# A scan kernel on one core: at step 3 of each unit TensorE sums the last state of the unit before ahead of delta's products, and ScalarE copies y behind the decay of chunk 4

## The chip, the cores and the metric

One core of a Trainium2 chip runs the whole kernel. The metric is the device time of one execution in microseconds; 3 executions of the kernel before were timed.

## The reference, cut to what matters

A bidirectional state-space block over 4 sequences of 1024 tokens with 1024 inner channels and N = 16 states. For each direction (z is the projected input of the direction, B and C come from a small projection):

```
delta = softplus(Wdt @ dlt + bdt)
h[t]  = exp(delta * A_n) * h[t-1] + delta * B_n * z      (n = 0..15, scan over t)
y     = sum over n of (C_n * h) + Dp * z
out   = Wf @ (silu(mx) * (y1 + y2)) + bf + skip ; result = x + gate * out
```

## The kernel before, in words

A set-up part of about 260 us makes the normalised tokens, folded weights and projections. The rest is 64 **units**, k = 0..63: unit k is one tile of 128 channels of one direction of one sequence, with all 1024 tokens in the free dimension. Units come in groups of 8 (one sequence and direction). Each unit has 16 **steps**, c = 0..15, one for each state n; q = 16 k + c numbers them through and "chunk" c is the work of state c. Each engine has its own list, written out by hand in the loops `for k ... for c`, and works it strictly in order; the lists meet at semaphores.

The way a state's inflow (delta B z) is made depends on the letter of `KINDS = "EVEVAVAPAVAPAPAV"`: for E TensorE multiplies by a diagonal into `slot` (L900), for A ScalarE scales `dut` into `abuf` (L1123, `scale_half`) and TensorE transposes that into `slot` (L888, `turn_inflow`), for V and P GpSimd multiplies a loaded B by `du` into `bst` (L1222). For E and A the decay goes into the one buffer `dec`, for V and P into `slot`. In each step:

- ScalarE makes the decay exp(delta A_n) (L1184). For an E or A chunk it first waits until the scan of the E or A chunk before has read `dec`.
- VectorE scans (L1314); for V it also multiplies by C (L1319), for the others GpSimd does (L1227).
- TensorE sums: `sum_chunk(q - LAG)`, LAG = 4, adds the transposed product of four steps ago into the PSUM tile `y` (L877, 8 transposes of 128x128). A scan waits until the sum five chunks back has left its buffer in `hbuf` (HR = 5).

So the sums of chunks 12 to 15 of unit k-1 stand in steps 0 to 3 of unit k. Behind the last of them `copy_y(k-1)` on ScalarE moves `y` to `yrd` (L1114, waits for the semaphore `summed`), and only then `skip_terms(k)` on TensorE (L870, step 4, waits for `y_read`) may start the next `y`, in front of the sum of chunk 0. The next unit's delta is prepared meanwhile: `delta_product(k+1)` in step 3 (L837, four products of 512 columns into the PSUM tile `mb`, each half waiting for the last user of its half of `mb`), on ScalarE `softplus_start` in step 4 (L1079 and L1081) and `softplus_end` in step 5 (L1085), on VectorE `finish_delta` in step 5 (L1248).

What else lies in the first steps depends on the unit. Units 2-9, 18-25, 34-41 and 50-57 follow one in which the gate branch was made (`has_mx`, L858, sigmoid on ScalarE L1098 to L1106, silu L1268). Units 26-33, 42-49 and 58-63, and unit 17, follow one whose output projection spans the border: 32 products of 128 columns in step 15 and 32 in step 0 (L958, L963), read by L1284. Units 10-15 have 8 products of 512 columns of a small projection in the same places (L951, L1154). The first unit of a group (8, 16, 24, ...) makes a new diagonal on ScalarE (L1139). In unit 63 there is no delta to prepare, and further projections stand in steps 1 to 4.

ScalarE's list around the change, for one step c:

```python
nc.scalar.activation(decays, delta[:, k % 2, :], ACT.Exp, ...)      # decay of chunk c
if c in SCALE_STEPS: scale_half(...)
...
if c == LAG - 1 and k > 0: copy_y(k - 1)                            # step 3
if k + 1 < NU:
    if c == 4: softplus_start(k + 1)
    if c == 5: softplus_end(k + 1)
```

Of the kernel before, what the change touches and what calls it, by code (L numbers as in the profile page):

```python
# [24 lines left out]
NU = 2 * B * ET  # L25
# [456 lines left out]
LAG = 4  # L482
# [5 lines left out]
def kind(q):  # L488

    return KINDS[q % N]
# [20 lines left out]
def ssm_kernel(nc, t, scratch):  # L513

    with ExitStack() as ctx:
# [67 lines left out]
        def gates(k):  # L583

            return k > 0 and backward(k - 1)

        def has_mx(k):
            return not gates(k) and k % (2 * ET) != 0

        def mx_index(k):  # L590

            return k // (2 * ET) * ET + (ET - 1 if backward(k) else k % ET - 1)
# [8 lines left out]
        def dbc_job(k):  # L601

            return k - ET - 1 if ET < k < ET + 1 + NC - 2 else None
# [220 lines left out]
        def _(pe):  # L824
            def delta_product(k):
                pe.wait_ge(wdt_in[k % 2], 16 * (k // 2 + 1))
                pe.wait_ge(dl_in, 48 * (k // ET + 1))
                for h in range(2):
                    if k >= 2 and has_mx(k - 2):
                        pe.wait_ge(silu_ready, 2 * mx_index(k - 2) + h + 1)  # L830
                    elif k >= 2 and dbc_job(k - 2) is not None:
                        pe.wait_ge(dbc_ready, 2 * dbc_job(k - 2) + h + 1)
                    elif k >= 2 and h == 0 and projection_of(k - 2) is not None:
                        pe.wait_ge(proj_read, projection_of(k - 2) + 1)
                    elif k >= 1:
                        pe.wait_ge(dut_ready, 2 * k - 1 + h)
                    nc.tensor.matmul(mb[h], wdt[:, k % 2, :], dl[:, half(h)], start=True, stop=True).then_inc(dps_mm, 1)  # L837
# [36 lines left out]
            def sum_chunk(q):  # L874
                wait_product(pe, q)
                for j in range(ET):
                    last = nc.tensor.matmul(y[:, j * P:(j + 1) * P], hbuf[:, q % HR, j * P:(j + 1) * P], ident[:],  # L877
                                            start=False, stop=(q % N == N - 1), is_transpose=True,
                                            skip_group_check=True)
                last.then_inc(summed, 1)  # L880
# [127 lines left out]
            for k in range(NU):  # L1008
                e, zs = k % ET, z_step(k)
                new_b = (k + 1) % ET == 0  # L1010
                for c in range(N):
                    q = N * k + c
                    if kind(q) == "A":
                        turn_inflow(q)
                    elif kind(q) == "E":
                        spread_inflow(q)
                    if c == 3 and k + 1 < NU:
                        delta_product(k + 1)
                    if c == LAG:
                        skip_terms(k)  # L1020
                    if q >= LAG:
                        sum_chunk(q - LAG)
                    if c == 0 and k > 0 and has_mx(k - 1):
                        mx_part(k - 1, 1, range(2, DT))
                    if c == 0 and k > 0 and dbc_job(k - 1) is not None:
                        pe.wait_ge(dut_ready, 2 * k + 2)
                        make_dbc(dbc_job(k - 1), 1)
                    if c == 0 and k > 0 and projection_of(k - 1) is not None:
                        project(projection_of(k - 1), mb[0], range(ET // 2, ET))
                    if c == 7 and gates(k):  # L1030
                        transpose_y(k - 1)
                    if k + 1 < NU:
                        if zs <= c < zs + 4:
                            z_part(k + 1, (c - zs) // 2, range((c - zs) % 2 * 2, (c - zs) % 2 * 2 + 2))
                        if c == zs + 4 and new_b:
                            turn_b((k + 1) // ET)
                        if c == (zs + 5 if new_b else zs + 4):
                            turn_du(k + 1, 0)
                        if c == zs + 6:
                            turn_du(k + 1, 1)  # L1040
                    if has_mx(k) and c >= 13:
                        mx_part(k, (c - 13) // 2, range((c - 13) % 2 * 2, (c - 13) % 2 * 2 + 2))
                    if c == 15 and dbc_job(k) is not None:
                        pe.wait_ge(dut_ready, 2 * (k + 1) + 1)
                        make_dbc(dbc_job(k), 0)
                    if c == 15 and projection_of(k) is not None and k + 1 < NU:
                        pe.wait_ge(dut_ready, 2 * (k + 1) + 1)
                        project(projection_of(k), mb[0], range(0, ET // 2))
                    if k == NU - 1 and c == 1:
                        pe.wait_ge(dut_ready, 2 * NU)  # L1050
                    if k == NU - 1 and 1 <= c <= 4:
                        project(projection_of(k), mb[1], range(2 * (c - 1), 2 * c))
                    if k == NU - 1 and 9 <= c <= 14:
                        for i in range(TAIL, TAIL + 2):
                            project_last(i, (c - 9,))
                    if k == NU - 1 and c == 15:
                        for i in range(TAIL, TAIL + 2):
                            project_last(i, (ET - 2,))
# [11 lines left out]
        def _(act):  # L1070
# [37 lines left out]
            def copy_y(k):  # L1108
                act.wait_ge(summed, N * (k + 1))
                if k > 0 and backward(k - 1):  # L1110
                    act.wait_ge(ytr_mm, 2 * pair(k - 1) + 2)
                elif k > 0:
                    act.wait_ge(y_out, 16 * (pair(k - 1) + 1))
                nc.scalar.activation(yrd[:], y[:], ACT.Copy).then_inc(y_read, 1)  # L1114
# [52 lines left out]
            for k in range(NU):  # L1167
                f, zs = wtile(k), z_step(k)
                new_b = (k + 1) % ET == 0
                for c in range(N):  # L1170
                    q = N * k + c
                    if c == 0:
                        act.wait_ge(delta_ready, k + 1)
                    if kind(q) in "AE":
                        if before("AE", q) > 0:
                            act.wait_ge(scanned, TURNED[before("AE", q) - 1] + 1)
                        decays = dec[:]
                    else:
                        if q >= 2:
                            wait_scanned_out(act, q - 2)  # L1180
                        elif q == 1:
                            act.wait_ge(bt_ready, 1)
                        decays = slot[q % 2][:]
                    nc.scalar.activation(decays, delta[:, k % 2, :], ACT.Exp,  # L1184
                                         scale=par[:, f // ET, f % ET, PA + c:PA + c + 1]).then_inc(decay_ready, 1)
                    if c == 0 and k > 0 and k % ET == 0:
                        make_diagonal(k // ET, 1)
                    if c in SCALE_STEPS:
                        scale_half(N * k + SCALE_STEPS[c][0], SCALE_STEPS[c][1])
                    if c == 1 and k > 0 and has_mx(k - 1):  # L1190
                        sigmoid_half(k - 1, 1)
                    if c in (0, 1) and k > 0 and dbc_job(k - 1) is not None:
                        evict_dbc(dbc_job(k - 1), c)
                    if c == LAG - 1 and k > 0:
                        copy_y(k - 1)
                    if k + 1 < NU:
                        if c == 4:
                            softplus_start(k + 1)
                        if c == 5:
                            softplus_end(k + 1)  # L1200
                        if c in (zs + 2, zs + 4):
                            skip_half(k + 1, (c - zs - 2) // 2)
                        if c == zs + 4 and new_b:
                            copy_bt((k + 1) // ET)
                        if c == 14 and new_b:
                            make_diagonal((k + 1) // ET, 0)
                        if c == zs + 5:
                            copy_dut(k + 1, 0)
                        if c == min(zs + 7, N - 1):
                            copy_dut(k + 1, 1)  # L1210
                    if c == 15 and has_mx(k):
                        sigmoid_half(k, 0)
# [202 lines left out]
```

## Time and profile before

| | |
|---|---|
| median of 3 executions | 3355.72 us (3354.21 to 3358.06) |
| the profiled execution | 3349.5 us, its span 3347.7 us |
| busy: TensorE, VectorE, ScalarE, GpSimd | 91%, 90%, 80%, 87% of the span |
| mean granted clock of TensorE | 0.975 of 2.4 GHz |

Timeline rows give start and duration in us, engine, line, operation, output and inputs, the count of merged instructions, and in brackets the idle time of the engine ahead of them with what ended it. VectorE's instructions overlap a little: a scan of 2.28 us lets the next one start 2.20 us after its own start. The copy of `y` (L1114) of unit k-1 marks step 3 of unit k; from one to the next is the time of a unit.

### The profile page before, as it was taken

What the parts mean: (1) busy time and instruction counts of PE and PEld (TensorE: products, weight loads), DVE (VectorE), ACT (ScalarE), POOL (GpSimd) and SP (SyncE); (2) the same over time, 40 slices, a digit from 0 to 9 for tenths busy, and PEclk for the clock granted to TensorE, in tenths of its full rate; (3) what the DMA queues carried; (4) which work ended last, traced back from release to release, by engine and by line L of the source; (5) the groups of instructions that cost most, each with busy time, mean ns of one, the idle gap of its engine ahead of it and who ended that gap; (6) DMA issues with size and microseconds to landing.
All of it is one profiled execution on the core that took longest, in us unless ns stands there. A gap on an engine that the chain in (4) does not pass through costs nothing.

```text
span 3347.7 us, 54862 instructions
## 1 busy us (share of the span) xinstructions
PE 3046.2 (91%) x19924; PEld 2391.0 (71%) x19924; DVE 3027.2 (90%) x2008; ACT 2680.3 (80%) x5134; POOL 2905.7 (87%) x1288
## 2 busy tenths in 40 slices
PE   8987999899989999899999999899999999898999
PEld 4555666667767667678787766678777666677789
DVE  2546999999999999999999999999999999999994
ACT  0346999988888999988777999988777999988772
POOL 1335999999999999999999999999999999999993
PEclk9988999999999999999999999999999999999999
DMA  5575334645457333644456334645466334644453
GB/s 224 172 266 170 125 125 138 232 134 168 161 197 244 123 129 133 223 142 156 156 197 224 127 129 133 228 138 161 149 200 228 127 124 137 228 134 159 151 195 112
DMA packets 206141, 560.40 MB, mean 167 GB/s; under 512 B 20184, under 2 KB 66456, under 8 KB 201520
## 3 DMA queue, kind: packets, MB, share of 16 engines
q1 hardware_dynamic: 203424, 538.01, 48.1%
q0 software_dynamic: 2304, 16.78, 1.3%
q8 instruction: 159, 2.61, 0.3%
q10 hardware_dynamic: 144, 2.10, 0.2%
q14 instruction: 110, 0.90, 0.1%
HBM read 476.19 MB, written 80.63 MB: 166 GB/s over the span
## 4 chain that ended last, share of the span: by engine, by line
PE 56%; ACT 20%; DVE 8%; issue 8%; POOL 1%; DVEq 0%; ACTq 0%; POOLq 0%
PE y L877 17%; PE slot L888 8%; PE mb L848 8%; ACT abuf L1123 7%; PE mb L958 6%; PE mb L858 5%; PE slot L900 5%; DVE hbuf L1314 4%; ACT dec L1184 4%; ACT slot L1184 3%; ACT soft L1079 2%; PE mb L837 2%; DVE slot L1314 2%; PE mb L951 1%; DVE delta L1248 1%
## 5 line engine op out<-in xcount | busy, mean ns | idle before, releaser
L1227 POOL TENSOR_TENSOR hbuf<-hbuf,cres 128x1024 f32<-128x1024 f32 x704 | 1663.6, 2378 | 179.2 <-DVE hbuf L1314 178.4
L1222 POOL TENSOR_TENSOR bst<-bst,du 128x1024 f32<-128x1024 f32 x512 | 1223.4, 2389 | 50.4 <-DVE du L1258 50.4
L1314 DVE TENSOR_TENSOR_SCAN hbuf<-dec,slot 128x1024 f32<-128x1024 f32 x512 | 1165.8, 2277 | 56.4 <-PE slot L900 32.7
L877 PEld LDWEIGHTS y<-ident,hbuf 128*128 128x128 f32 x8192 | 969.6, 145 | 137.9 <-issue 134.3
L877 PE MATMUL y<-ident,hbuf 128*128 128x128 f32 x8192 | 1066.3, 279 | 0.7 <-POOL hbuf L1227 0.7
L1123 ACT ACTIVATE abuf<-dut,bt 128x128 f32<-128x128 f32 x3072 | 970.9, 387 | 0.0
L1314 DVE TENSOR_TENSOR_SCAN slot<-slot,bst 128x1024 f32<-128x1024 f32 x320 | 729.1, 2278 | 43.5 <-ACT slot L1184 43.2
L1184 ACT ACTIVATE dec<-delta,par 128x1024 f32<-128x1024 f32 x512 | 584.7, 1142 | 123.0 <-DVE hbuf L1314 123.0
L1184 ACT ACTIVATE slot<-delta,par 128x1024 f32<-128x1024 f32 x512 | 566.6, 1107 | 118.7 <-DVE hbuf L1319 106.4
L888 PE MATMUL slot<-ident,abuf 128*128 128x128 f32 x3072 | 420.9, 282 | 168.6 <-ACT abuf L1123 148.2
L888 PEld LDWEIGHTS slot<-ident,abuf 128*128 128x128 f32 x3072 | 350.2, 144 | 299.5 <-ACT abuf L1123 224.1
L848 PE MATMUL mb<-xn,wzs 128*128 128x512 f32 x1008 | 478.9, 597 | 26.0 <-DVE delta L1248 15.0
L1314 DVE TENSOR_TENSOR_SCAN hbuf<-slot,bst 128x1024 f32<-128x1024 f32 x192 | 435.0, 2265 | 0.1
L1319 DVE TENSOR_TENSOR hbuf<-slot,cres 128x1024 f32<-128x1024 f32 x320 | 392.0, 1225 | 11.0
L848 PEld LDWEIGHTS mb<-xn,wzs 128*128 128x128 f32 x1008 | 172.8, 192 | 156.9 <-issue 156.9
L900 PEld LDWEIGHTS slot<-diag,dut 128*128 128x128 f32 x2048 | 244.8, 194 | 30.5 <-issue 27.8
L900 PE MATMUL slot<-diag,dut 128*128 128x128 f32 x2048 | 253.6, 278 | 10.5 <-DVE hbuf L1314 5.1
L858 PE MATMUL mb<-xn,wx 128*128 128x512 f32 x512 | 240.9, 593 | 0.0
L958 PE MATMUL mb<-ybuf,wf 128*128 128x128 f32 x1504 | 176.4, 275 | 2.2 <-ACT dut L1148 2.2
L958 PEld LDWEIGHTS mb<-ybuf,wf 128*128 128x128 f32 x1504 | 171.9, 192 | 2.7 <-ACT dut L1148 2.6
L440 PE MATMUL ps<-wz,wct 128*128 128x512 f32 x256 | 127.3, 638 | 21.1 <-DMA wct<-in_wcT 21.1
L837 PE MATMUL mb<-dl,wdt 81*128 81x512 f32 x256 | 125.2, 609 | 12.7 <-DVE silu L1268 8.4
(156 smaller groups left out, 2234.8 us busy)
## 6 DMA issues: line engine op xcount, KB each, us to landing
bst<-bc_s SPq DMA_DIRECT2D x512, 512.0 KB, 3.9
cres<-bc_s SPq DMA_DIRECT2D x128, 512.0 KB, 6.5
wzs<-wz_s SPq DMA_DIRECT2D x64, 256.0 KB, 4.2
yf_s<-yrd SPq DMA_DIRECT2D x32, 512.0 KB, 5.4
ybuf<-yf_s SPq DMA_DIRECT2D x32, 512.0 KB, 4.9
yg_s<-ybuf SPq DMA_DIRECT2D x31, 512.0 KB, 4.4
si_s<-silu SPq DMA_DIRECT2D x28, 512.0 KB, 6.1
silu<-si_s SPq DMA_DIRECT2D x28, 512.0 KB, 5.4
```

The costliest lines, as they stand in the source:

```text
L848: last = nc.tensor.matmul(z_bank(k, h), wz[:, i * P:(i + 1) * P], xn[:, h, i, :], start=(i == 0), stop=(i == DT - 1))
L858: last = nc.tensor.matmul(mb[h], wx[:, i * P:(i + 1) * P], xn[:, h, i, :], start=(i == 0), stop=(i == DT - 1))
L877: last = nc.tensor.matmul(y[:, j * P:(j + 1) * P], hbuf[:, q % HR, j * P:(j + 1) * P], ident[:], start=False, stop=(q % N == N - 1), is_tr ...
L888: last = nc.tensor.matmul(slot[q % 2][:, j * P:(j + 1) * P], abuf[:, a % 2, j * P:(j + 1) * P], ident[:], start=True, stop=True, is_transp ...
L900: last = nc.tensor.matmul(slot[q % 2][:, j * P:(j + 1) * P], dut[:, j * P:(j + 1) * P], diag[:, i, j, :], start=True, stop=True)
L958: nc.tensor.matmul(bank[:, m * P:(m + 1) * P], wf[:, e, m * P:(m + 1) * P], tokens, start=(e == 0 and m == 0), stop=False, skip_group_chec ...
L1123: last = nc.scalar.activation(abuf[:, a % 2, j * P:(j + 1) * P], dut[:, j * P:(j + 1) * P], ACT.Copy, scale=bt[:, g % 2, j, n:n + 1])
L1184: nc.scalar.activation(decays, delta[:, k % 2, :], ACT.Exp, scale=par[:, f // ET, f % ET, PA + c:PA + c + 1]).then_inc(decay_ready, 1)
L1222: nc.gpsimd.tensor_tensor(bst[:, i % BR, :], bst[:, i % BR, :], du[:, k % 2, :], ALU.mult).then_inc(pool_b, 1)
L1227: nc.gpsimd.tensor_tensor(hbuf[:, q % HR, :], hbuf[:, q % HR, :], cres[:, q % N, :], ALU.mult).then_inc(pool_prod, 1)
L1314: nc.vector.tensor_tensor_scan(h[:, ::step], decays[:, ::step], inflows[:, ::step], 0.0, ALU.mult, ALU.add).then_inc(scanned, 1)
L1319: nc.vector.tensor_tensor(hbuf[:, q % HR, :], slot[q % 2][:], cres[:, c, :], ALU.mult).then_inc(dve_prod, 1)
```

## The change

In step 3 TensorE's list has the sum of chunk 15 of unit k-1 first and the products of delta of unit k+1 second. ScalarE's list has the copy of `y` one place later: it stood at the end of step 3, ahead of the decay of chunk 4; it stands directly behind that decay. No instruction is added or removed.

```diff
                     elif kind(q) == "E":
                         spread_inflow(q)
-                    if c == 3 and k + 1 < NU:
-                        delta_product(k + 1)
                     if c == LAG:
                         skip_terms(k)
                     if q >= LAG:
                         sum_chunk(q - LAG)
+                    if c == 3 and k + 1 < NU:
+                        delta_product(k + 1)
...
                     nc.scalar.activation(decays, delta[:, k % 2, :], ACT.Exp,
                                          scale=par[:, f // ET, f % ET, PA + c:PA + c + 1]).then_inc(decay_ready, 1)
+                    if c == LAG and k > 0:
+                        copy_y(k - 1)
...
-                    if c == LAG - 1 and k > 0:
-                        copy_y(k - 1)
                     if k + 1 < NU:
                         if c == 4:
                             softplus_start(k + 1)
```

## Rows read from the trace of the kernel before

**Rows 1.** Waits of the whole span: who waited for whom, us in total, times, longest.
```profile
ACT yrd L1114 <- PE y L877: 84.0, 32, 9.1
...
DVE slot L1314 <- ACT slot L1184: 43.2, 69, 1.7
```
**Rows 2.** Timeline of ScalarE in unit 28, steps 3 to 5.
```profile
1596.90 1.02 ACT L1114 ACTIVATE yrd<-y 128x1024 f32<-128x1024 f32 x1 [2.87 <-PE y L877]
1597.82 1.14 ACT L1184 ACTIVATE dec<-delta,par 128x1024 f32<-128x1024 f32 x1
1598.86 1.02 ACT L1079 ACTIVATE soft<-mb 128x1024 f32<-128x1024 f32 x1
...
1600.87 1.10 ACT L1184 ACTIVATE slot<-delta,par 128x1024 f32<-128x1024 f32 x1
```
**Rows 3.** Timeline of VectorE in the same steps: scans of chunks 2, 3, 4, 5 and a product.
```profile
1593.48 2.29 DVE L1314 TENSOR_TENSOR_SCAN hbuf<-dec,slot 128x1024 f32<-128x1024 f32 x1 [0.78 <-ACT slot L1184]
1595.69 2.27 DVE L1314 TENSOR_TENSOR_SCAN slot<-slot,bst 128x1024 f32<-128x1024 f32 x1
...
1599.14 2.28 DVE L1314 TENSOR_TENSOR_SCAN hbuf<-dec,slot 128x1024 f32<-128x1024 f32 x1
1602.00 2.30 DVE L1314 TENSOR_TENSOR_SCAN slot<-slot,bst 128x1024 f32<-128x1024 f32 x1 [0.59 <-ACT slot L1184]
```
**Rows 4.** Timeline of TensorE in the same steps.
```profile
1594.10 1.88 PE L837 MATMUL mb<-dl,wdt 81*128 81x512 f32 x4
1595.82 1.04 PE L877 MATMUL y<-ident,hbuf 128*128 128x128 f32 x8
...
1598.06 1.06 PE L870 MATMUL y<-ident,ud 128*128 128x128 f32 x8 [0.33 <-ACT yrd L1114]
...
1603.22 1.09 PE L888 MATMUL slot<-ident,abuf 128*128 128x128 f32 x8 [2.35 <-ACT abuf L1123]
1604.15 3.55 PE L877 MATMUL y<-ident,hbuf 128*128 128x128 f32 x16
```
**Rows 5.** Timeline of ScalarE in unit 10: the copy of y.
```profile
751.50 1.02 ACT L1114 ACTIVATE yrd<-y 128x1024 f32<-128x1024 f32 x1 [1.03 <-PE y L877]
```
**Rows 6.** Timeline of unit 24, all engines: delta's products, the copy, scans of chunks 4, 5.
```profile
1403.10 2.07 PE L837 MATMUL mb<-dl,wdt 81*128 81x512 f32 x2 [2.11 <-DVE silu L1268]
...
1406.91 1.02 ACT L1114 ACTIVATE yrd<-y 128x1024 f32<-128x1024 f32 x1 [1.11 <-PE y L877]
...
1409.01 2.29 DVE L1314 TENSOR_TENSOR_SCAN hbuf<-dec,slot 128x1024 f32<-128x1024 f32 x1 [0.32 <-ACT dec L1184]
...
1412.02 2.30 DVE L1314 TENSOR_TENSOR_SCAN slot<-slot,bst 128x1024 f32<-128x1024 f32 x1 [0.72 <-ACT slot L1184]
```
**Rows 7.** Timeline of unit 19, all engines: steps 2 to 6 (the first row is the scan of chunk 2).
```profile
1171.04 2.28 DVE L1314 TENSOR_TENSOR_SCAN hbuf<-dec,slot 128x1024 f32<-128x1024 f32 x1
...
1173.46 1.06 PE L888 MATMUL slot<-ident,abuf 128*128 128x128 f32 x8
...
1174.26 1.00 ACT L1114 ACTIVATE yrd<-y 128x1024 f32<-128x1024 f32 x1
...
1175.41 1.07 PE L870 MATMUL y<-ident,ud 128*128 128x128 f32 x8 [0.89 <-ACT yrd L1114]
...
1176.31 1.91 PE L877 MATMUL y<-ident,hbuf 128*128 128x128 f32 x16
...
1179.34 2.30 DVE L1314 TENSOR_TENSOR_SCAN slot<-slot,bst 128x1024 f32<-128x1024 f32 x1 [0.39 <-ACT slot L1184]
```
**Rows 8.** Timeline of unit 63, all engines: the copy of y and the transposed inflow of chunk 4.
```profile
3254.62 1.02 ACT L1114 ACTIVATE yrd<-y 128x1024 f32<-128x1024 f32 x1 [4.72 <-PE y L877]
...
3256.21 1.04 PE L888 MATMUL slot<-ident,abuf 128*128 128x128 f32 x8
```
**Rows 9.** Windows: stretch, its length, busy us (instructions) of five engines, granted clock, DMA.
```profile
1602.00:1608.00 6.00, 4.78 (x28) 4.78 (x29) 5.96 (x4) 6.00 (x14) 4.26 (x2) 0.72 0.25 92
```
**Rows 10.** Timeline of unit 8, TensorE: delta's second half in front of the last sum.
```profile
655.78 1.12 PE L837 MATMUL mb<-dl,wdt 81*128 81x512 f32 x2 [2.10 <-DVE silu L1268]
```

## The prediction

> **What bounds the kernel now.** I read the page's engine shares first: no engine has more than 91%, VectorE has 90%, so who waits for whom decides. Then the table of waits: ScalarE's copy of y waited 84.0 us in 32 places for TensorE's sums, and VectorE's scan stood 43.2 us in 69 places behind a decay written to `slot` [rows 1]. Then the list of all 64 copies of y in the timeline, which sorts the units. Last, the first six steps of one unit of each sort, engine by engine.
>
> Two sorts matter. In **border units** (22 with a projection at the border: 17, 26-33, 42-49, 58-62; and 6 with the small projection, 10-15) the copy waits. Unit 28 stands for the 22: ScalarE idles 2.87 us, copies y at 1596.90, then makes the decay of chunk 4 (1597.82), two softplus passes (1598.86 and the one behind), and the decay of chunk 5 at 1600.87, which ends at 1601.97 [rows 2]. The scan of chunk 5 starts then, at 1602.00, after 0.59 us of idle; the scan of chunk 4 started 2.86 us earlier, where unhindered scans stand 2.21 us apart (1593.48 to 1595.69) [rows 3]. The reader is to see that the whole run from the copy to the decay of chunk 5 is one chain on ScalarE without a gap, and that it hangs on the last sum: delta's products start at 1594.10, the sum behind them at 1595.82, done at 1596.86 [rows 4]. The decay of chunk 4 needs only the end of the scan of chunk 2, 1593.48 + 2.29 = 1595.77, to have `dec` free [rows 3]. It is queued behind a copy that comes 1.1 us later.
>
> In the **32 other units** (1-9, 16, 18-25, 34-41, 50-57, less 24 and 40) the copy finds its sum done; in unit 19 it runs at 1174.26 with no idle ahead of it, since ScalarE itself is late there, and the scan of chunk 5 still idles 0.39 us [rows 7].
>
> **TensorE's swap.** The sum needs nothing that is late: chunk 15 is a V chunk, multiplied by VectorE a step before. It starts where delta's products start now, so 1595.82 - 1594.10 = 1.72 us sooner: done near 1595.15 in unit 28. Delta's products move back by one sum, 0.87 us (eight transposes of 1.04 us overlapping the next group), and end near 1596.85 [rows 4]. Who waits for them is the first softplus pass, which comes near 1597.8 (below), so they stay hidden by 1 us; without that cover each 0.1 us would cost 0.1 us per unit. The transposed inflow of chunk 4 follows at the same time as before. In the units with a silu at the border the products waited for it with the sum behind them; now the sum isn't held up. By itself the swap frees the copy from 1595.15, but ScalarE's chain gains only down to where the scan lets it.
>
> **ScalarE's move, with the swap.** In unit 28 the decay of chunk 4 starts at 1595.77 + 0.09 = 1595.86 (the 0.09 is how long ScalarE's other waits for a scan last from its end), inside what was idle. The copy follows 1.04 us later at 1596.90, just where it stood; the softplus passes start 0.92 us behind it, at 1597.82 instead of 1598.86, and everything behind is 1.04 us sooner: the decay of chunk 5 ends at 1600.93. The scan of chunk 5 could start at 1599.14 + 2.20 = 1601.34. So the decay has 0.4 us to spare and the stall is gone: 1602.00 - 1601.34 = 0.66 us, and 0.03 us more because a scan that starts from idle hands over 0.03 us later. **0.69 us per border unit.** The other 0.35 us of ScalarE's 1.04 falls on nothing. What is late next: nothing in this unit before chunk 8, where ScalarE waits for a scan, and GpSimd and TensorE also restart from VectorE in steps 6 to 8, so the shift passes through to the unit's end; the two other stalls of VectorE at chunks 0 and 2 (0.56 and 0.78 us, the latter in [rows 3]) hang on products that start from VectorE's own du, and stay. `skip_terms` waits for the same copy at the same time.
>
> In unit 10 ScalarE idles only 1.03 us, because the scan of chunk 2 is as much later; the decay goes into that gap and the copy again keeps its place near 751.50, and the 0.59 us stall of chunk 5, the same as unit 28's, goes [rows 5]. So 28 units, of which unit 27 gives only 0.34 us (its stall reads 0.23): 27 x 0.69 + 0.34 = 19.0 us.
>
> Unit 24: TensorE idles 2.11 us on silu, then delta's second half and the sum run at half rate, the copy waits 1.11 us, and scans of chunks 4 and 5 idle 0.32 and 0.72 us [rows 6]. With the sum first the gap is cut by a sum and the copy waits for nothing; ScalarE's chain is 1.1 us sooner and both stalls go, 1.1 us. Unit 40 has the same with a copy wait of 0.16 us: 0.2 us. Unit 63 makes no delta; its copy waits 4.72 us for a sum that doesn't move, and chunk 4's scan for a transposed inflow at 3256.21 [rows 8]: 0. The tail: 0.
>
> **The other 32 units.** ScalarE's chain has no idle, so swapping two of its links changes neither its end nor chunk 5's decay: 0 gained, the 0.39 us stall stays. The decay of chunk 4 starts at 1174.26, behind the scan of chunk 2 (1171.04 + 2.28 = 1173.32): no new wait. But the copy is one decay later, 1.04 us: `skip_terms` goes from 1175.41 to 1176.45, with the sums of chunks 0 and 1 queued behind it, and SyncE's store of y, which delays no load of B since the next one waits for the scan of chunk 5. The sum of chunk 0 ends at 1176.31 + 1.04 + 1.04 = 1178.4; the scan of chunk 5 needs it at 1179.34 [rows 7]. Hidden, with 0.95 us to spare. Cost 0.
>
> **Sum:** 19.0 + 1.1 + 0.2 = 20.3 us. The profiled execution (3349.5 us, span 3347.7 us) would read 3329; it lies 6 us under the median of 3355.72, so the median becomes **3335.4 us**, -0.6%. A measurement of this kernel can tell about 0.2%, 6.7 us.
>
> **The weak spot: TensorE's clock.** In unit 19 TensorE's idle in front of `skip_terms` grows from 0.89 to 1.93 us (1173.46 + 1.06 to 1176.45) [rows 7], and the 2.35 us one in front of the next transposed inflow shrinks to 1.3. In 31 of 60 units the gap of 2.34 or 2.35 us is followed by transposes at 1.2 GHz, half rate: unit 28's 16 transposes took 3.55 us instead of 1.91 [rows 4, 7], and the mean granted clock over 1602 to 1608 was 0.72 of 2.4 GHz [rows 9]. That costs nothing, as the scan of chunk 6 is 2 us away. After gaps of 2.1 us the clock had fallen in unit 24 and hadn't in unit 8 [rows 6, 10]; of six between 2.04 and 2.18 us three fell, of the four of 1.45 to 1.77 us none. The new 1.93 us lies between. If the clock falls, `skip_terms` and the sum of chunk 0 take up to 0.87 us longer each, less the 0.95 us to spare: 0.8 us per unit.
>
> The Trainium skill (TensorE: Matmul & The Clock Gate, Part 4: PE-mode transpose) says that transposes don't count as busy for the gate; then all of steps 4 to 6 would look idle to it and the fall would be the rule: 0.8 us in all 32 units, 3335 + 26 = 3361 us. The trace speaks against it: in the same steps long rows of transposes run at full rate in 29 of 60 units.
>
> **Rivals.** (A) As above, 3335.4, chance 0.73; its own range 3332 to 3340: below, the stall at chunk 2 gives a little too; above, 0.59 instead of 0.69 us and 1 us less for unit 24, and the scatter of a median (2 us). (B) The clock falls in the new gap: in half of the 32 units 16 x 0.8 = 13 us lost, 3348. Chance 0.12. (C) The slower side, one mechanism: it falls in all 32, 26 us lost against 20 gained, 3361; it decides from the 26th unit on (20.3 / 0.8). If half rate also holds up the sum of chunk 1 it is a few us more. Chance 0.03. (D) The stall at chunk 5 is paid again at the next wait, so the change does nothing: 3356. For it speaks that GpSimd has 19 instructions of 2.4 us in every unit, 45 of 48 us; against it that it idles in steps 5 and 6 of border units. Chance 0.08. (E) The freed TensorE time also shortens the stall of the other units: 28 x 0.39 = 11 us more, 3324. Nothing in ScalarE's chain shortens, chance 0.04.
>
> **Numbers.** Faster by over 0.2% (under 3349): A, E and over half of B, 0.84. Within: D and the rest of B and part of C, 0.13. Slower: 0.03. The range 3330 to 3349 leaves out E, most of C and D and part of B, 0.17.
>
> **What would show it.** In unit 28's place: the decay of chunk 4 ahead of the copy, the copy without or with under 0.1 us of wait, the scan of chunk 5 with no idle; a border unit 47.4 instead of 48.1 us, unit 19's kind 45.7 as before with 0.39 us at chunk 5. ScalarE's waits for the sum fall from 84.0 to some 15 us. It is wrong if chunk 5's scans in unit 19's kind idle 1 us or more behind TensorE (the clock), or if border units idle more at chunks 0, 2 or 6.

## The result, and the profile after

The changed kernel took 3343.68 us (median of 6 executions, 3339.1 to 3347.55) against 3356.89 us for the kernel before; the ratio is 0.9959 with a 95% interval of 0.9946 to 0.9972. It is 13 us faster; 20 were forecast. In a second session the same kernel (run e4 below) had a ratio of 0.9975 (0.9965 to 0.9984). The profiled execution was 3343.68 us, its span 3341.9 us. The profile before had a span of 3347.7 us and lay some 7 us under the median of its kernel, so the two profiles differ by 5.8 us only, where the medians differ by 13.

The table of waits of the kernel after (who waited for whom, us in total, times, longest) has what answers to [rows 1], TensorE's wait for the copy, which was 35.2 us in 59 places before, and a wait that is new:

```profile
PE y L870 <- ACT yrd L1114: 67.9, 62, 1.9
...
DVE slot L1314 <- ACT slot L1184: 22.6, 30, 1.7
...
DVE slot L1314 <- PE y L877: 13.6, 14, 1.2
...
ACT yrd L1114 <- PE y L877: 9.1, 1, 9.1
```

The copy's wait for the last sum is gone but for the very last one (84.0 us in 32 places before; some 15 us were forecast), and VectorE's wait for decays in `slot` fell by 20.6 us. But 14 scans of chunk 5 wait for TensorE's sum of chunk 0, 13.6 us in all, which none did before.

**A border unit.** Unit 28, ScalarE's timeline after:

```profile
1593.24 1.15 ACT L1184 ACTIVATE dec<-delta,par 128x1024 f32<-128x1024 f32 x1 [1.78 <-DVE hbuf L1314]
1594.29 1.00 ACT L1114 ACTIVATE yrd<-y 128x1024 f32<-128x1024 f32 x1
1595.20 1.01 ACT L1079 ACTIVATE soft<-mb 128x1024 f32<-128x1024 f32 x1
...
1597.21 1.10 ACT L1184 ACTIVATE slot<-delta,par 128x1024 f32<-128x1024 f32 x1
```

and VectorE's:

```profile
1596.57 2.28 DVE L1314 TENSOR_TENSOR_SCAN hbuf<-dec,slot 128x1024 f32<-128x1024 f32 x1
1598.76 2.27 DVE L1314 TENSOR_TENSOR_SCAN slot<-slot,bst 128x1024 f32<-128x1024 f32 x1
```

The decay of chunk 4 now comes first, the copy follows without a wait, and the scan of chunk 5 starts 2.19 us behind that of chunk 4, with no idle, where [rows 3] have 2.86. From its scan of chunk 0 to the next unit's, unit 28 lasts 47.42 us instead of 48.11, unit 10 lasts 46.69 instead of 47.40.

**A unit after a silu unit.** Unit 4, TensorE's timeline after (steps 4 to 6):

```profile
472.51 1.06 PE L888 MATMUL slot<-ident,abuf 128*128 128x128 f32 x8
475.51 1.94 PE L870 MATMUL y<-ident,ud 128*128 128x128 f32 x8 [1.93 <-ACT yrd L1114]
477.24 2.56 PE L877 MATMUL y<-ident,hbuf 128*128 128x128 f32 x16
```

the windows view there (stretch, length, busy us and instructions of TensorE, its weight loads, VectorE, ScalarE, GpSimd, then granted clock, DMA share, GB/s):

```profile
474.00:476.00 2.00, 0.49 (x3) 0.52 (x4) 1.97 (x3) 2.00 (x3) 2.00 (x2) 0.79 0.20 49
476.00:478.00 2.00, 2.00 (x11) 2.00 (x10) 2.00 (x1) 1.97 (x3) 2.00 (x2) 0.50 0.97 291
```

and VectorE's timeline:

```profile
475.73 2.28 DVE L1314 TENSOR_TENSOR_SCAN hbuf<-dec,slot 128x1024 f32<-128x1024 f32 x1
479.07 2.30 DVE L1314 TENSOR_TENSOR_SCAN slot<-slot,bst 128x1024 f32<-128x1024 f32 x1 [1.06 <-PE y L877]
```

The gap in front of `skip_terms` is 1.93 us, as worked out from [rows 7], and over 476 to 478 the granted clock is 0.50: 1.2 of 2.4 GHz. `skip_terms` takes 1.94 instead of 1.07 us, the sum of chunk 0 behind it is late, and the scan of chunk 5 idles 1.06 us instead of 0.39. The unit lasts 46.32 us instead of 45.65. There are 28 gaps of 1.93 us in front of L870. Behind 19 of them `skip_terms` or the sum of chunk 0 runs at half rate, wholly or in part; in 9 of these the clock falls only as `skip_terms` ends and the scan isn't held up, in the other 10 it is. The hits come in every second unit or so (4, 6; 34, 36; 51, 53, 55). In the kernel before, the falls came later in the unit, behind the gap of 2.35 us in front of chunk 6's transposes, and cost nothing; that gap is now 1.31 us and none follows it.

**Units 8, 24, 40 and 56.** The other 4 of the 14 scans are in these four units, where delta's second half waits for silu, and here the clock is low before `skip_terms` is reached. With the sum ahead of delta's products nothing stands between the wait for silu and the next transposed inflow but delta's second half, so the one gap of 2.1 us of before ([rows 6], [rows 10]) has become two. Unit 8 after, TensorE and the scan of chunk 5:

```profile
657.75 1.13 PE L837 MATMUL mb<-dl,wdt 81*128 81x512 f32 x2 [1.23 <-DVE silu L1268]
660.03 1.94 PE L888 MATMUL slot<-ident,abuf 128*128 128x128 f32 x8 [1.16 <-DVE hbuf L1314]
662.55 1.94 PE L870 MATMUL y<-ident,ud 128*128 128x128 f32 x8 [0.58 <-ACT yrd L1114]
...
666.33 2.30 DVE L1314 TENSOR_TENSOR_SCAN slot<-slot,bst 128x1024 f32<-128x1024 f32 x1 [0.80 <-PE y L877]
```

Each of these four units lasts 47.9 us; units 8 and 56 lasted 47.09 us before.

**The first unit of a late group.** In unit 48 TensorE's projection starts late:

```profile
2524.13 6.59 PE L958 MATMUL mb<-ybuf,wf 128*128 128x128 f32 x32 [3.17 <-issue]
```

VectorE's scan of chunk 0 idles 6.45 us there, against 1.99 in the profile before. The trace shows what the projection waits for: the load of the gated tile `ybuf` (L702) lands at 2524.04, 0.09 us ahead of it, and in all eight profiles the projections of units 32 and 48 start 0.09 to 0.23 us behind that landing. The load took 7.2 to 10.2 us from issue to landing, differently each time. The clock is in this wait too: it fell within the gap of 3.17 us, and the 32 products took 6.59 us, where they took 3.81 us in unit 48 of the kernel before. This wait was in every profile taken, with 1.99 to 6.84 us in unit 48 and 1.18 to 4.20 in unit 32; the five longest of the sixteen, 4.14 us and more, are those in which the clock fell.

### The profile page after: what moved, and what is told of

Read it like the earlier page. It is cut to its first block, busy times and chain, and to the rows that moved or that the text cites. A ratio compares the mean times of both kernels' runs of the same rounds, so it can differ in the third digit from the quotient of the medians.

```text
span 3341.9 us, 54862 instructions
## 1 busy us (share of the span) xinstructions
PE 3042.9 (91%) x19924; PEld 2372.2 (71%) x19924; DVE 3023.9 (90%) x2008; ACT 2680.1 (80%) x5134; POOL 2904.7 (87%) x1288
## 4 chain that ended last, share of the span: by engine, by line
PE 40%; ACT 22%; DVE 17%; issue 12%; POOL 1%; DVEq 0%; ACTq 0%; POOLq 0%
PE y L877 12%; DVE hbuf L1314 9%; ACT abuf L1123 8%; PE slot L888 7%; PE mb L848 5%; ACT slot L1184 5%; PE mb L858 4%; DVE slot L1314 4%; PE mb L958 4%; PE slot L900 3%; ACT dec L1184 3%; DVE delta L1248 2%; DVE hbuf L1319 2%; PE mb L951 1%; ACT soft L1079 1%
## 5 line engine op out<-in xcount | busy, mean ns | idle before, releaser
L877 PE MATMUL y<-ident,hbuf 128*128 128x128 f32 x8192 | 1043.5, 277 | 0.7 <-POOL hbuf L1227 0.7
L877 PEld LDWEIGHTS y<-ident,hbuf 128*128 128x128 f32 x8192 | 952.3, 144 | 104.5 <-issue 103.4
L888 PEld LDWEIGHTS slot<-ident,abuf 128*128 128x128 f32 x3072 | 342.2, 142 | 259.7 <-issue 132.9
L888 PE MATMUL slot<-ident,abuf 128*128 128x128 f32 x3072 | 410.3, 277 | 88.3 <-ACT abuf L1123 55.4
L858 PE MATMUL mb<-xn,wx 128*128 128x512 f32 x512 | 240.9, 593 | 0.0
L870 PE MATMUL y<-ident,ud 128*128 128x128 f32 x512 | 78.9, 304 | 67.9 <-ACT yrd L1114 67.9
```

Of the source, the lines that this page charges most:

```text
L858: last = nc.tensor.matmul(mb[h], wx[:, i * P:(i + 1) * P], xn[:, h, i, :], start=(i == 0), stop=(i == DT - 1))
L888: last = nc.tensor.matmul(slot[q % 2][:, j * P:(j + 1) * P], abuf[:, a % 2, j * P:(j + 1) * P], ident[:], start=True, stop=True, is_transp ...
```

## Experiments

Two theories of the missing 7 us were set against each other: the clock in the new gap, or the late projections of units 32 and 48. The runs e1 to e4 shared a chip and 14 runs of the kernel before (3358.45 us), e5 and e6 another session (9 runs, 3356.76 us).

**e1: the swap alone.** The copy stays in step 3.

```diff
-                    if c == 3 and k + 1 < NU:
-                        delta_product(k + 1)
                     if c == LAG:
                         skip_terms(k)
                     if q >= LAG:
                         sum_chunk(q - LAG)
+                    if c == 3 and k + 1 < NU:        # moved here, as in the change
+                        delta_product(k + 1)
... (ScalarE's list, as before)
                     if c == LAG - 1 and k > 0:
                         copy_y(k - 1)
```

> TensorE's swap alone; the copy of y stays in step 3, in front of the decay of chunk 4. Theory 1 (the shortfall against the forecast is TensorE's clock falling in the 1.93 us gap in front of skip_terms, which the later copy makes in the units after a silu unit): the gap is 0.89 us again, no scan of chunk 5 waits for TensorE, border units still last 47.4 instead of 48.1 us since the sum is out of the copy's way; about 20 us faster than before, ratio 0.994, and 5 to 8 us faster than both halves together. Theory 2 (the shortfall is the late load of gated tiles in units 32 and 48, which comes and goes by itself): the same time as both halves together, 0.996.

Measured: 3338.06 us, ratio 0.9943 (0.9931 to 0.9956). TensorE in unit 5, and the windows view there:

```profile
520.23 1.07 PE L888 MATMUL slot<-ident,abuf 128*128 128x128 f32 x8
522.18 1.07 PE L870 MATMUL y<-ident,ud 128*128 128x128 f32 x8 [0.89 <-ACT yrd L1114]
523.08 1.91 PE L877 MATMUL y<-ident,hbuf 128*128 128x128 f32 x16
```

```profile
522.00:524.00 2.00, 1.82 (x17) 1.85 (x18) 1.97 (x3) 1.99 (x3) 2.00 (x2) 1.00 0.37 76
```

The gap is 0.89 us, the clock full, and after none of the 28 such gaps is it low. No scan of chunk 5 waits for TensorE. In the border units the copy still waits 1.14 us (2.87 before) and that is enough:

```profile
1590.93 1.02 ACT L1114 ACTIVATE yrd<-y 128x1024 f32<-128x1024 f32 x1 [1.14 <-PE y L877]
1591.85 1.14 ACT L1184 ACTIVATE dec<-delta,par 128x1024 f32<-128x1024 f32 x1
```

Unit 30 lasts 47.41 us, as with both halves. So the swap alone brings the whole gain of the change. The clock still falls behind 17 of the 31 gaps of 2.35 us that are left in front of chunk 6's transposes, and behind the two gaps of units 8, 40 and 56, and no scan waits for it: a fall costs only where the later copy has used up the room. Theory 1 as expected, though the distance to both halves on the same chip (run e4) is 11.7 us where 5 to 8 were expected; theory 2 fails, since unit 48 idles 5.75 us here too.

**e2: the copy's move alone.** Delta's products stay in front of the last sum.

```diff
                     nc.scalar.activation(decays, ...).then_inc(decay_ready, 1)
+                    if c == LAG and k > 0:
+                        copy_y(k - 1)
...
-                    if c == LAG - 1 and k > 0:
-                        copy_y(k - 1)
```

> ScalarE's move alone; delta's products stay in front of the last sum. Both theories: border units gain the same 0.69 us, since the decay of chunk 4 fits into the copy's wait: 19 us. Theory 1: the gap of 1.93 us is there, scans of chunk 5 wait for TensorE in 12 to 16 of the 32 other units, unit 24 gains less than with the swap: 10 to 12 us faster in all, ratio 0.9965. Theory 2: no such waits, the ratio differs from that of both halves only by units 24 and 40, 1 us.

Measured: 3348.58 us, ratio 0.9965 (0.9953 to 0.9977). ScalarE in unit 28, and the row of waits:

```profile
1600.33 1.15 ACT L1184 ACTIVATE dec<-delta,par 128x1024 f32<-128x1024 f32 x1 [1.78 <-DVE hbuf L1314]
1601.42 1.02 ACT L1114 ACTIVATE yrd<-y 128x1024 f32<-128x1024 f32 x1
```

```profile
DVE slot L1314 <- PE y L877: 16.3, 16, 1.2
```

The decay goes into the copy's wait, unit 28 lasts 47.41 us. Border units gain as much as with the swap: each half removes the same stall alone. But 16 scans wait for TensorE, 13 of them behind gaps of 1.93 us, where theory 1 wanted 12 to 16 and theory 2 none. This half brings the loss. Units 24 and 56 are among the 16 behind a gap of only 1.45 us in front of `skip_terms`, with one of 2.10 us some 5 us earlier.

**e3: both halves, the gap filled.** In 35 units (the 28 with the gap of 1.93 us and the first of each group but the very first) TensorE issues the transposes of chunk 4's inflow twice, into the same place; it does more work for the same result.

```diff
+                again = 2 if c == LAG and k > 0 and (has_mx(k - 1) or k % ET == 0) else 1
-                for j in range(ET):
+                for j in list(range(ET)) * again:
                     last = nc.tensor.matmul(slot[q % 2][:, j * P:(j + 1) * P], abuf[...], ident[:], ...)
```

> Both halves, and in the 34 units that follow no border work the 8 transposes of chunk 4's inflow are issued twice into the same place, which fills 0.87 us of TensorE's gap in front of skip_terms (1.93 becomes 1.06) and delays nothing that is due. Theory 1: the clock no longer falls there, no scan of chunk 5 waits for TensorE, about 8 us faster than both halves alone: 3335 us, ratio 0.994, although TensorE does more. Theory 2: no change against both halves, 0.996, or slower by the added work where it matters.

Measured: 3341.69 us, ratio 0.9947 (0.9934 to 0.9959), against 0.9975 for both halves on the same chip. TensorE and VectorE in unit 5:

```profile
526.65 1.94 PE L890 MATMUL slot<-ident,abuf 128*128 128x128 f32 x16
529.65 1.06 PE L870 MATMUL y<-ident,ud 128*128 128x128 f32 x8 [1.06 <-ACT yrd L1116]
```

```profile
532.54 2.30 DVE L1316 TENSOR_TENSOR_SCAN slot<-slot,bst 128x1024 f32<-128x1024 f32 x1 [0.39 <-ACT slot L1186]
```

The copy stands where it stands in the changed kernel and `skip_terms` starts no sooner; only the gap is filled, and no scan waits for TensorE. So neither the late copy nor the later sum costs anything by itself; the clock behind the gap does. This is the run that settles it. What it can't separate is the length of the gap from the work done ahead of it, as the filling changes both. The median lies 7 us above the 3335 expected by theory 1. The table below shows where: the first scan comes 9 us later than in the profile before, in the set-up part, and unit 32 idles 4.20 us instead of 1.18.

**e4: both halves again.** The changed kernel as it is.

> The changed kernel itself, on the same chip as its neighbours, as their measure. Both theories: ratio 0.996 as measured before. Theory 1: scans of chunk 5 wait for TensorE in 10 to 18 units, not the same ones as before; theory 2: the total differs with the waits of TensorE for gated tiles in the first units of groups.

Measured: 3349.78 us, ratio 0.9975 (0.9965 to 0.9984), 1.6 thousandths above the first session. The waits:

```profile
DVE slot L1314 <- PE y L877: 16.2, 16, 1.2
```

16 units again, partly others than before (3, 5, 7, 9 in place of 4, 6, 8). The ratio expected, 0.996, is just outside the interval. Of the 4.7 us between the two profiles of this kernel 3.9 are in the set-up part.

**e6: half the filling.** Four of the eight transposes are issued twice (`for j in [*range(again), *range(ET)]` with `again` 4 or 0), so that the gap is about 1.5 us.

> Both halves, and 4 of the 8 transposes of chunk 4's inflow issued twice in the same units: TensorE's gap in front of skip_terms is 1.93 - 0.43 = 1.5 us. If the clock falls by the length of this gap as in the kernel before (none of the four gaps of 1.45 to 1.77 us), no scan of chunk 5 waits for TensorE: ratio 0.9945, as with the whole filling. If falls fade out slowly with the gap: a quarter of the units still lose 0.8 us, 0.996.

Measured: 3335.2 us, ratio 0.9936 (0.9923 to 0.9948). TensorE in unit 5, and the windows view:

```profile
518.41 1.50 PE L890 MATMUL slot<-ident,abuf 128*128 128x128 f32 x12
521.40 1.06 PE L870 MATMUL y<-ident,ud 128*128 128x128 f32 x8 [1.49 <-ACT yrd L1116]
```

```profile
522.00:524.00 2.00, 2.00 (x21) 1.97 (x19) 1.90 (x1) 1.97 (x3) 2.00 (x2) 1.00 0.90 285
```

After none of the 28 gaps of this length is the clock low, against some 20 of 28 at 1.93 us; the falls don't fade out slowly with the gap. One scan of chunk 5 waits for TensorE, in unit 24, behind the two gaps of 1.24 and 1.16 us at the silu. This version and e1 are faster than the kernel before and, by their intervals, than both halves as e4 has them; the intervals of the two overlap each other.

**e5: the swap alone, and two softplus passes one step later.** An attempt on the 0.39 us stall that is left.

```diff
-                        if c == 4:
-                            softplus_start(k + 1)
                         if c == 5:
+                            softplus_start(k + 1)
                             softplus_end(k + 1)
```

> The swap alone, and ScalarE's two first softplus passes move from step 4 to step 5, behind the decay of chunk 5 and the scaling, directly in front of the third pass. If the 0.39 us stall of chunk 5 in the 28 units after a silu unit is ScalarE's order alone, it goes (the decay ends 0.9 us before the scan could start) and each of these units lasts 45.2 instead of 45.7 us: 12 us faster than the swap alone, ratio 0.9905. Rival: ScalarE has no slack behind it, and the stall comes back as a wait for the decay of chunk 6, 7 or 8 or for delta: the same time as the swap alone, 0.994. Border units: no change, 47.4 us.

Measured: 3344.46 us, ratio 0.9961 (0.9947 to 0.9974). The stall of chunk 5 went, and one at chunk 0 came. TensorE and VectorE at the border to unit 20:

```profile
1207.67 1.88 PE L858 MATMUL mb<-xn,wx 128*128 128x512 f32 x4
1209.39 1.95 PE L900 MATMUL slot<-diag,dut 128*128 128x128 f32 x16
```

```profile
1211.43 2.29 DVE L1313 TENSOR_TENSOR_SCAN hbuf<-dec,slot 128x1024 f32<-128x1024 f32 x1 [0.57 <-issue]
```

The scan starts as the inflow of chunk 0 ends (1209.39 + 1.95 = 1211.34), and TensorE comes to that without a gap from step 14. These units last 45.85 us, those of e1 45.66 to 45.74: the rival holds in that the gain was paid back at another wait, though at chunk 0 behind TensorE and not at one of the places it named. In units 9, 25, 41 and 57, without the gate's products (L858) at their end, the gain of 0.5 us stayed (46.67 to 46.17 us in unit 25); units 8, 24, 40 and 56 lost 0.6 us and units 17, 33 and 49 0.7 us each. What makes TensorE's run start later in e5 was not tested.

The time from the first scan to that of unit 63, split by sort of unit (sums of the distances between scans of chunk 0; units 31 and 47, whose ends hold the waits of 32 and 48, by themselves; the 35 others take in unit 0 and units 8, 24, 40 and 56), and ahead of it where the first scan starts. From the first scan of unit 63 to the end it is 103.5 us in every profile.

| | first scan | 26 border units | units 31, 47 | 35 others |
|---|---|---|---|---|
| before | 283.3 | 1244.5 | 100.4 | 1613.7 |
| both halves | 284.0 | 1226.3 | 104.3 | 1621.4 |
| both halves, again | 287.9 | 1226.6 | 103.6 | 1622.6 |
| swap alone (e1) | 285.9 | 1226.8 | 102.7 | 1612.9 |
| copy alone (e2) | 288.7 | 1226.6 | 102.5 | 1623.3 |
| gap filled (e3) | 292.2 | 1227.0 | 102.4 | 1612.4 |
| half filled (e6) | 284.1 | 1227.3 | 100.6 | 1612.6 |
| swap, softplus later (e5) | 286.0 | 1228.6 | 104.0 | 1618.1 |

The last column sorts the kernels by theory 1: 1621 to 1623 us with the later copy and nothing in the gap, 1612 to 1613 without the one or with the other.

## Why the prediction was right or wrong

**Right.** The sign, and the stated range of 3330 to 3349 holds the 3343.68 us of the first session (the second had 3349.8, on a chip on which the kernel before was 3358.45). Rival A, the forecast itself with a chance of 0.73, isn't what came: its own range ended at 3340, and the prediction's sign of being wrong, scans of chunk 5 that idle 1 us or more behind TensorE in the other units, stood in 7 of them. The range holds because it had room for a part of rival B. The mechanism in the border units was right to a hundredth: 0.69 us were worked out for each, and 48.11 - 47.42 = 0.69 was measured in unit 28, 0.71 in unit 10, 0.35 against 0.34 in unit 27; the 26 in the table gave 18.2 us. What would be late next there was right too: nothing; the stalls at chunks 0 and 2 stayed at 0.56 and 0.78 us. The gap of 1.93 us, the gap of 1.3 us behind it, the other units' 0.39 us at chunk 5 where the clock holds, and the price of 0.8 us per unit at half rate were also as said: a fully hit unit in e4 lasted 46.50 instead of 45.66 us.

**Wrong: "Hidden, with 0.95 us to spare. Cost 0."** This term, the later `skip_terms` in the 32 other units, is the step that failed. It was given at full rate, and the fall of the clock in the new gap had a chance of only 0.12, as rival B, and 0.03, as C. It happened: behind 19 of the 28 gaps of 1.93 us the clock was at half rate, 10 scans were held up there, 4 more in units 8, 24, 40 and 56, and the other units took 1621.4 - 1613.7 = 7.7 us more, 8.9 in e4. B's size for half of the units, 13 us, was too large: fewer scans were held up, and most of them for less than 0.8 us, as the clock fell or came back within the two groups of transposes. With the measured 8 us taken from the 20 the forecast would have been 3343. The evidence for it was at hand: a gap of 2.11 us with a fall [rows 6], and three falls in the six gaps just over 2 us. It had been weighed by the nearest gaps below, of which there were four.

**Wrong next to it: units 8, 24, 40 and 56.** Units 24 and 40 were to give 1.1 and 0.2 us, and 8 and 56 were counted with the other units, though they wait for silu as well. The copy's wait and the stall at chunk 4 went as said, and "the gap is cut by a sum" was right; but a second gap of 1.16 us opened behind it, which the prediction doesn't have, and the clock fell behind the two in all four units: 47.92 instead of 48.24 us in unit 24, 47.90 instead of 47.30 in unit 40, 0.8 us more in 8 and 56, each with 0.8 us at chunk 5. In e1, without the later copy, units 24 and 40 last 47.02 and 47.10, though in unit 40 the clock falls there too: there the whole gain is seen.

**The sentence about what ScalarE's move brings.** The working took both halves together. Taken alone, each removes the same stall, so the second one adds nothing to the border units, and the later copy then adds only the gap. The prediction said of the swap that it "frees the copy from 1595.15" and stopped there; worked out to the end it would have shown that the other half had no gain left to bring.

**The rivals.** C (all 32 units) and D (nothing moves) did not come, nor did E: the stall of chunk 5 in the other units is 0.39 us wherever the clock holds. The Trainium skill (TensorE: Matmul & The Clock Gate, Part 4: PE-mode transpose) says that the full clock doesn't engage for transposes, as they don't count as busy in the same way. The prediction weighed this against the trace and rejected it, and e6 bears that out: in unit 5 TensorE ran nothing but transposes from 518.41 to 529.13 us of the span, and the granted clock was 1.00 throughout. What falls is tied to the gaps.

**Left open.** The load of the gated tile lands late for units 32 and 48 and leaves TensorE idle for 0.7 to 3.9 us, differently in each profile; why was not tested. There is one profile of each kernel but the changed one, and the profile before has the shortest waits in both units (one tied with e1's), so a share of the change in them isn't excluded. This and the set-up part make each total uncertain by some us, and with it the exact share of the 7 us that the clock took. In the first session's two profiles this wait alone has 4.5 us more in unit 48, of which 2.8 are its products at half rate. What, besides its length, decides whether a gap brings a fall is open too: e2 has it behind 1.45 us and e4, behind the same length, has not.

## What to carry to other kernels

When a copy or a wait is moved "for free", work out the gap it leaves on TensorE and not only the slack of what follows: this one had 0.95 us of slack and lost it to half rate. Count the gaps ahead of it as well: in units 8, 24, 40 and 56 the clock was low before the moved copy was reached. If two edits remove the same wait, try each alone; here the swap kept the gain and left out the cost of the other. A few repeated transposes into a place that is written anyway held the clock up here, where TensorE would only have been idle.

## What the runs showed of the hardware

- TensorE's clock: behind gaps of 1.93 us in this place it fell to 1.2 GHz in 19 of 28 (after), 21 of 28 (e2) and 20 of 28 (e4); behind gaps of 0.89 (e1), 1.06 (e3) and 1.49 us (e6) in none of 28 each. Two of three gaps of 1.45 us in e2, with one of 2.10 us some 5 us earlier, were followed by a fall, and none of two in e4.
- Added work made the kernel faster: 8 more transposes in each of 35 units, 0.9947 against 0.9975 on one chip.
- With nothing but transposes on TensorE for 10 us, and gaps of 1.49 and 1.31 us between them, the granted clock stayed at 1.00 (e6, unit 5).
- Two gaps of 1.23 and 1.16 us with a microsecond of work between were followed by half rate as well: in unit 8 of the kernel after the next transposes (L888) took 1.94 instead of 1.06 us. This place was followed by a fall in 4 of 4 units after, 3 of 4 in e1 and in e3, 2 of 4 in e4, e5 and e6.
